# Causal-mask products by row groups, and block-scale steps moved from VectorE to ScalarE with new instruction orders, in a fused tokeniser, attention and feed-forward kernel

## The reference, cut to what matters

```
q, k = rotary(rmsnorm(x Wq)), rotary(rmsnorm(x Wk))      # 16 half heads of 16
scores = where(causal, q k / 4, -inf); attn = softmax(scores)
out = layernorm((attn[even] - lam * attn[odd]) v) * (1 - LAMBDA_INIT)
h2 = x + out Wproj
# feed-forward on layernorm(h2), every operand rounded in blocks of 16:
scale = max(max|block| / 6, 1e-12); q = grid(block / scale) * scale   # fp4 grid
y = h2 + (silu(q(x) q(Wg)) * (q(x) q(Wu)) -> q) q(Wd)     # 256 -> 704 -> 256
```

## Time and profile before

| | |
|---|---|
| median of 3 runs | 519.29 us (517.73 to 519.75) |
| profiled execution | 516.11 us, its span 514.4 us |
| granted TensorE clock, mean | 0.996 of full |
| busy PE / DVE / ACT / POOL | 483.8 / 465.5 / 327.7 / 263.7 us |

### The profile page before, as it was taken

One profiled execution on the slowest core, in us unless ns is written; L12 is line 12 of the kernel. 1 busy time (PEld: TensorE's weight loads), 2 busy tenths in 40 slices (PEclk: granted clock), 3 DMA queues, 4 the chain that ended last, 5 costly groups with the idle time before them and its releaser, 6 DMA issues.

```text
span 514.4 us, 13552 instructions
## 1 busy us (share of the span) xinstructions
PE 483.8 (94%) x3642; PEld 392.1 (76%) x3642; DVE 465.5 (91%) x1275; ACT 327.7 (64%) x752; POOL 263.7 (51%) x359
## 2 busy tenths in 40 slices
PE   4998998999999999999999979899999999999996
PEld 3776675677777777777776657798888888888895
DVE  4788989999999999999989799999999999999984
ACT  5787667687777877777776868554454454544531
POOL 4345545656454554454546245654565446556542
PEclk9999999999999999999999989999999999999999
DMA  8911101111111111111121111221212121121111
GB/s 283 351 50 44 34 2 38 58 46 50 55 54 48 48 47 49 54 52 48 48 61 43 48 39 30 60 63 51 61 42 60 52 61 52 50 61 53 51 45 56
DMA packets 31842, 32.12 MB, mean 62 GB/s; under 512 B 4160, under 2 KB 30016, under 8 KB 31808
## 3 DMA queue, kind: packets, MB, share of 16 engines
q1 hardware_dynamic: 31808, 31.72, 20.8%
HBM read 22.99 MB, written 8.71 MB: 62 GB/s over the span
## 4 chain that ended last, share of the span: by engine, by line
PE 47%; DVE 32%; issue 13%; DMA 2%; SPq 2%; ACT 1%; DVEq 1%; POOL 1%; POOLq 0%; ACTq 0%
PE bank L156 14%; PE bank_a L156 6%; PE bank L806 5%; PE bank L818 5%; DVE bank L1288 4%; PE bank L797 4%; DVE fh L1239 3%; DVE fh L1271 3%; PE bank L711 3%; DVE fh L1245 3%; PE bank L831 2%; PE bank_b L849 2%; DVE bank L1257 2%; DVE fx L1300 2%; DMA wproj_raw<-in_wproj_t 2%
## 5 line engine op out<-in xcount | busy, mean ns | idle before, releaser
L894 ACT ACTIVATE pt<-bank 113x452 f32<-113x452 f32 x128 | 61.0, 553 | 36.8 <-PE bank L806 36.8
L1361 POOL TENSOR_TENSOR h_deq<-fh,fhb 128x704 f32<-128x704 f32 (+1 forms) x29 | 39.6, 1366 | 62.2 <-DVE fhb L1213 61.0
L156 PE MATMUL bank<-wgu_hi,fx_hi 128*128 128x512 f32 x168 | 64.3, 383 | 1.8 <-DVE fx_lo L1280 1.8
L156 PE MATMUL bank<-wgu_hi,fx_lo 128*128 128x512 f32 x168 | 63.7, 379 | 0.0
L156 PE MATMUL bank<-wgu_lo,fx_hi 128*128 128x512 f32 x168 | 63.5, 378 | 0.0
L971 POOL TENSOR_TENSOR rope<-rope 113x512 f32<-113x512 f32 x32 | 41.0, 1283 | 30.3 <-DVE rope L1010 30.0
L964 POOL TENSOR_TENSOR rope<-rope,columns 113x256 f32<-113x256 f32 x64 | 48.2, 771 | 13.6 <-DVE rope L1002 13.1
L156 PE MATMUL bank_a<-wd_hi,fh_hi 128*128 128x256 f32 x168 | 49.8, 296 | 0.6 <-DVE fh_lo L1233 0.5
L156 PE MATMUL bank<-wqkv_hi,xo_hi 128*113 128x256 f32 (+1 forms) x128 | 46.6, 364 | 1.7 <-DVE rope L1002 1.5
L156 PE MATMUL bank_a<-wd_lo,fh_hi 128*128 128x256 f32 x168 | 46.9, 279 | 0.0
L156 PE MATMUL bank_a<-wd_hi,fh_lo 128*128 128x256 f32 x168 | 46.9, 279 | 0.0
(11 more groups left out here) (202 smaller groups left out, 1492.0 us busy)
## 6 DMA issues: line engine op xcount, KB each, us to landing
xb<-h_dram SPq DMA_DIRECT2D x29, 129.0 KB, 2.1
h_dram<-h SPq DMA_DIRECT2D x32, 112.9 KB
rb<-h_dram SPq DMA_DIRECT2D x28, 128.0 KB, 2.1
out<-res SPq DMA_DIRECT2D x28, 128.0 KB, 1.7
px<-in_patches SPq DMA_DIRECT2D x9, 384.0 KB, 9.2
hx<-in_txt SPq DMA_DIRECT2D x32, 77.0 KB
hr<-in_txt SPq DMA_DIRECT2D x32, 77.0 KB
h_dram<-y SPq DMA_DIRECT2D x9, 128.0 KB, 1.9
```

The costliest lines, as they stand in the source:

```text
L156: last = pe.matmul(dst, a(k), w(k), start=(start and n == 0), stop=(n == len(passes) - 1))
L894: act.activation(pt[0:T, r, :, :].rearrange("p s t -> p (s t)"), sc_ps[r][0:T, :], ACT.Exp, scale=1.0 / math.sqrt(HD)).then_inc(m["exp_mad ...
L1361: pool.tensor_tensor(blocks(of(h_deq, s), BLK), blocks(of(h_code, s), BLK), spread(of_blocks(h_scale, s), BLK), ALU.mult).then_inc(f["h_de ...
```

## The change

Masks: the mask tile becomes `late_16`, 32-row groups each holding the mask of four blocks of queries. The product is cut by query block g and row group r: 16 products with a contraction over 32 rows (17 in the last block).

```diff
-                for r in range(NG):
-                    pe.matmul(sc_ps[r][0:T, :], ident_16[0:T, 0:T], mask_16[0:T, :], start=True, stop=True)
+                if isinstance(s, int) and s == 0:
+                    pe.wait_ge(k["late_ready"], NG + 1)
+                for g in range(NG):
+                    queries = slice(g * ROW, min((g + 1) * ROW, T))
+                    wide = queries.stop - queries.start
+                    for r in range(NG):
+                        rows = slice(r * ROW, r * ROW + wide)
+                        pe.matmul(sc_ps[r][0:T, :].rearrange("p (s t) -> p s t", t=T)[:, :, queries], late_16[rows, g, :],
+                                  ident_16[rows, rows].unsqueeze(1).broadcast_to([wide, GS, wide]),
+                                  start=(g == 0), stop=True, skip_group_check=True)
```

Making the mask moves behind `b1_wide` on POOL, as one memset and four selections of 32 rows; PE's first wait no longer asks for it:

```diff
-            pool.memset(mask_16[:], 0.0).then_inc(k["ident_ready"], 1)
-            pool.wait_ge(k["ident_ready"], 9)
-            key_late = mask_16[0:T, :].rearrange("p (s t) -> p s t", t=T)
-            pool.affine_select(out=key_late, in_=key_late, compare_op=ALU.is_ge, fill=MASKED, base=0,
-                               pattern=[[0, GS], [1, T]], channel_multiplier=-1).then_inc(k["ident_ready"], 1)
             pool.wait_ge(k["columns_loaded"], 16)
             pool.tensor_copy(b1_wide[:], spread(columns[:, KP:2 * KP], P)).then_inc(k["b1_spread"], 1)
+            pool.memset(late_16[:], 0.0).then_inc(k["late_ready"], 1)
+            pool.wait_ge(k["late_ready"], 1)
+            for r in range(NG):
+                late = late_16[r * ROW:(r + 1) * ROW]
+                pool.affine_select(out=late, in_=late, compare_op=ALU.is_ge, fill=MASKED, base=0,
+                                   pattern=[[ROW, NG], [-1, T]], channel_multiplier=1).then_inc(k["late_ready"], 1)
+            pool.wait_ge(k["late_ready"], NG + 1)
```

```diff
+            def x_shorts(s):
+                ...
+                act.wait_ge(f["x_amax"], s + 1)
+                after(act, f["x_short"], s)
+                act.activation(x_over[:], x_amax[:], ACT.Relu, bias=below[:], scale=SHORT / 6.0).then_inc(f["x_over"], 1)
+                act.wait_ge(f["x_over"], s + 1)
+                after(act, f["x_inv"], s)
+                after(act, f["x_scaled"], s)
+                act.activation(x_short[:], x_over[:], ACT.Identity, bias=least[:]).then_inc(f["x_short"], 1)
+            def x_scales(s):
+                act.wait_ge(f["x_short"], s + 1)
+                after(act, f["x_deq"], s)
+                act.activation(x_scale[:], x_short[:], ACT.Copy, scale=-1.0 / SHORT).then_inc(f["x_scaled"], 1)
```

Orders: all lists from the transition on are new; the attention loop's are as before. The rounds of the feed-forward loop:

```diff
 SP
-                    (3, load), (-4, store), (-3, load_residual)))
+                    (4, load), (-4, store), (-3, load_residual)))
 DVE
-                    (-3, h_low), (2, x_maxima), (-4, rows_out), (2, x_inverse), (0, hidden), (-1, h_rounded),
-                    (1, x_low), (-1, h_codes), (2, x_rounded), (-1, h_scales), (2, x_codes), (0, h_maxima),
-                    (2, x_scales), (0, h_inverse)))
+                    (-1, hidden), (1, x_rounded), (-1, h_maxima), (1, x_codes), (-2, h_rounded),
+                    (-1, h_inverse), (-4, rows_out), (-3, h_low), (3, x_maxima), (-2, h_codes), (1, x_low),
+                    (3, x_inverse)))
 POOL
-                    (-2, h_dequantise), (1, x_dequantise), (-1, h_quotient), (2, x_quotient)))
+                    (2, x_quotient), (1, x_dequantise), (-1, h_quotient), (-2, h_dequantise)))
 ACT
-                    (-3, h_high), (2, x_norm), (0, silu), (-1, h_magnitude), (1, x_high), (2, x_magnitude)))
+                    (-1, h_shorts), (3, x_norm), (-3, h_high), (2, x_scales), (0, silu), (1, x_high),
+                    (3, x_shorts), (2, x_magnitude), (-1, h_magnitude), (-1, h_scales)))
 PE
-                    (0, first_columns), (0, middle_columns), (0, last_columns), (-2, h_transposes), (1, x_transposes), (-3, down)))
+                    (-4, down), (0, first_columns), (-3, h_transposes), (0, middle_columns), (1, x_transposes),
+                    (0, last_columns)))
```

More of the change, by code:

```diff
@@ L1318, in ffn_vector @@
-            return steps, namedtuple("FfnVector", "rows_out h_low h_rounded h_codes h_scales x_maxima x_inverse hidden x_low h_maxima h_inverse x_rounded x_codes x_scales")(rows_out, h_low, h_rounded, h_codes, h_scales, x_maxima, x_inverse, hidden, x_low, h_maxima, h_inverse, x_rounded, x_codes, x_scales)
+                    (-1, hidden), (1, x_rounded), (-1, h_maxima), (1, x_codes), (-2, h_rounded),
+                    (-1, h_inverse), (-4, rows_out), (-3, h_low), (3, x_maxima), (-2, h_codes), (1, x_low),
@@ L1339, in vector_transition @@
-            a.residual(30, 0); f.x_codes(3); f.x_scales(3); a.out_sums(30, 0); f.x_maxima(4); a.out_variance(30, 0)
-            f.x_inverse(4); f.h_rounded(1); f.hidden(2); f.x_low(3); f.h_codes(1); a.newton_step(35, 1)
-            f.h_scales(1); f.x_rounded(4); f.h_maxima(2); a.xo_low(36, 0); f.h_inverse(2); f.x_codes(4); f.h_low(0)
-            a.residual(31, 1); f.x_scales(4); a.out_sums(31, 1); f.x_maxima(5); a.out_variance(31, 1)
-            f.x_inverse(5); f.h_rounded(2); f.x_low(4); f.hidden(3); f.h_codes(2); a.newton_step(36, 0)
@@ L1344, in vector_transition @@
-            f.h_scales(2); f.h_maxima(3); f.h_inverse(3); f.x_rounded(5); f.h_low(1); f.x_codes(5); f.rows_out(0)
-            f.x_scales(5); f.hidden(4); f.h_rounded(3); f.h_codes(3); f.x_maxima(6); f.x_inverse(6); f.x_low(5)
-            f.h_scales(3); f.h_maxima(4); f.x_rounded(6); f.x_codes(6); f.x_scales(6); f.h_inverse(4)
+            a.out_variance(24, 0); a.ln_sums(31, 1); a.xo_low(30, 0); a.newton_step(29, 1); a.o_apply(26, 0)
+            a.scale_qk(29, 1); a.ln_variance(31, 1); a.ratios(27, 1); a.mix_product(27, 1); a.mix_sum(27, 1)
@@ new lines, in vector_transition @@
+            a.newton_step(35, 1); f.x_inverse(4); f.h_maxima(1); a.xo_low(36, 0); f.h_rounded(0); f.h_inverse(1)
+            f.x_maxima(5); f.x_low(3); a.residual(31, 1); a.out_sums(31, 1); a.out_variance(31, 1); f.h_codes(0)
+            f.hidden(2); f.x_rounded(4); f.x_codes(4); a.newton_step(36, 0); f.h_maxima(2); f.x_inverse(5)
+            f.h_rounded(1); f.h_inverse(2); f.h_low(0); f.x_low(4); f.h_codes(1); f.hidden(3); f.x_rounded(5)
+            f.x_codes(5); f.x_maxima(6); f.h_maxima(3); f.x_inverse(6); f.h_rounded(2); f.h_inverse(3)
@@ L1348, in ffn_gpsimd @@
+            f.rows_out(0); f.h_low(1); f.x_maxima(7); f.h_codes(2); f.x_low(5); f.x_inverse(7)
         def ffn_gpsimd(pool):
@@ L1809, in pipeline @@
             transition(engine, stages, tile_stages)
-            with engine.Fori(5, 24) as t:
+            with engine.Fori(5, 23) as t:
                 tiles(t)
```

252 lines of the change are left out of this document (130 added, 122 removed).

## The result

The changed kernel takes 512.38 us (median of 4 runs, 511.79 to 513.33), the kernel before 518.84 (4 runs, 517.73 to 519.75). The ratio is 0.9876 with a 95% interval of 0.9845 to 0.9908: faster by 1.2%. The forecast was 508.3, with a range of 503.0 to 517.5. The profiled execution took 512.66 us with a span of 510.9; that of before took 516.11 with 514.4.

What follows compares the result with a forecast made beforehand. PE was taken to bound the attention loop and DVE the feed-forward loop. Terms 2.7 + 1.4 + 5.9 + 1.8 - 0.5 - 0.3 = 11.0 us, off the 519.29 median, gave 508.3 us, range 503 to 517.5.

Steps and rivals of the forecast that it cites:

- its main term: Feed-forward loop: moved steps and new orders cut a tile from 7.24 to 6.92 us, gaining 5.9 us.
- the tightest ring: Feed-forward loop: waits from `h_maxima` through ACT and DVE back to it, 6.6 us, covered by PE's 6.92.
- The other terms: Gains of 2.7 and 1.4 from masks and 1.8 in the passage; losses of 0.5 at the start, 0.3 at the end.
- a kept pace: Rival, feed-forward loop: the tile stays at 7.24 us, 5.9 us is gone, total 514.2; 16 in 100.
- a ring slower than 7.24: Rival, feed-forward loop: the ring through `h_shorts` closes at 7.7 us, total 522.8; 9 in 100.
- the attention loop is PE's with DVE 0.19 behind: Attention loop: PE sets 7.02 us a sequence, and DVE lets only 0.19 us of any PE gain through.
- The terms 2.7 and 1.4: Mask gains: 2.7 us over the 18 looped sequences, 1.4 us over the other 14.
- The masks' price: Sixteen new mask products a sequence: 0.55 us taken, against 0.78 for the old four.
- The rival that they cost as much as the scores: Masks at the scores' 0.97 us add 0.19 a looped sequence on PE; total 517.2, no difference; 12 in 100.
- The passage: Between attention and feed-forward loops, 258 to 326 us: DVE spared small operations, 1.8 us gain counted.
- The end: Last stage: two ACT operations replace one on DVE for tiles 27 and 28, 0.3 us lost (0 to 1).
- The base: Whole kernel: 3.2 us added from the profiled 516.1 to the runs' median 519.29, moving 505.1 to 508.3.

Runs made afterwards that it cites:

- e1: The kernel before with only the new mask products and the mask made behind `b1_wide`; 518.26 us, ratio 0.9997 to the kernel before.
- e5: The changed kernel with its sixteen mask products issued three times over; 518.39 us in one run, the kernel before 517.19.
- e6: The changed kernel with `xo_high` copying only half its chunks in the attention loop, part of the computation left out; 511.3 us.
- e12: The changed kernel with the mask made ahead of `b1_wide`, `rope_sum(30)` ahead of `x_quotient(0)`, and filling transposes in passage and end; 509.17 us.
- e4: The changed kernel with the mask made ahead of `b1_wide`, as in the kernel before; 512.9 us.
- e10: The changed kernel with 11 filling transposes on TensorE ahead of `h_transposes(28)` at the end; 511.11 us.
- e9: The changed kernel with steps kept on ScalarE but the feed-forward orders of the kernel before on every engine; 569.69 us.
- e8: The changed kernel with its new orders, but the short and scale steps of the feed-forward part back on VectorE; 530.68 us.

## Why the prediction was right and where it failed

**The call, faster by over 0.5%, was right, and by its main term.** The feed-forward loop was DVE's, the moved steps and the new orders together hand it to PE, and the tile takes 6.89 us (forecast 6.92). 5.9 us were forecast and 6.3 came. The 5.9 was the old loop's 18.8 tiles times 0.32, which is 6.0. The price of ACT's six operations, the floor of PE, the tightest ring being covered, the later first `w_quotients` and that no table is loaded again in the loop were right. (That ring adds up to 6.7 with the 0.59 of `x_norm`, not to 6.6, and the prediction's 1.5 us from the Trainium skill's forms for the six operations is 1.64 by those forms; 1.71 came.) The other terms were to give 5.1 together; in the profiles they came to -2.8. That the measured median lies only 4.1 us above the forecast is owed in part to the base, as told below, and that part is luck. The rivals of a kept pace and of a ring slower than 7.24 fall with the 6.89.

**The failed step is "the attention loop is PE's with DVE 0.19 behind".** It rested on a chain of waits through PE alone. The loop is a ring through PE, ACT and DVE of 7.0 us, and PE's own work just filled it: the new masks take up to 0.26 us off PE and that changed nothing (e1), 0.45 more of them cost 0.22 (e5), and an ACT copy shorter by 0.19 gave 0.11 back until DVE's list held it (e6). The terms 2.7 and 1.4 hung on it; of 4.1 us some 0.4 at most came, start included. The profile of before had the row that would have told it: `xo_low` (L1025) ends at 207.92 and `project` starts at 207.98. I read only DVE's own idle time, and not who waits for DVE.

**The masks' price** was bounded from 0.40 to 0.97 and taken at 0.55. Their own row has 0.35; with the 0.09 by which they start later behind `qk_transposes` and the 0.08 or more by which `project` follows `pv_transposes` later, it is 0.52 or more, and PE's gain is 0.26 at most where 0.23 was forecast. So the term was sized well, and it was the path that gave nothing. By the Trainium skill's floor of about 25 ns between starts (TensorE: Matmul & The Clock Gate, Part 1) the sixteen alone would take 0.40 us; here they take 0.35, 22 ns each, and in e5 the 32 further ones take 0.45, 14 ns each; the chain has no 62 ns per product either. The prediction set its 0.2 us beside the drain at a change of tiling mode of which the Trainium skill, TensorEngine Tiling (Array Packing), Key Properties, speaks; that section gives no duration, so the two could not agree in size. The rival that they cost as much as the scores was wrong on that, and the outcome would have been the same had it been right within the shadow.

**The passage** was to gain 1.8 and lost 1.0, 1.7 for equal work. DVE had less to do there (61.13 us in place of 64.75 from 258 to 330 us), but the chain ran over ACT's table loads, POOL's quotient and a clock that was at its lower level twice and not once. e12's 70.8 us show that about 2 of these are to be had.

**The end** was to lose 0.3 and lost 2.2 in the profile, 1.4 of it in `down(27)` at the lower clock. Another 0.66 is `h_transposes(24)`, which the kernel before does ahead of the cut, so 0.1 is left. By the same cut e4 and e10 to e12 lose 0.2 to 0.5, less than those 0.66. So the two ACT operations cost nothing that shows here, and the low clock came in four of eight such profiles.

**The base.** The forecast went from one execution to the median of the runs by adding 3.2. It left open what made the difference, and the clock fits: over all chips the runs of the kernel before with a mean clock of 0.996 have spans of 514.5 to 515.5 us, those with 0.986 519.1 to 520.3. Its profiled execution was one of the first kind, the changed kernel's (0.99) wasn't. By the profiles 3.5 of the 11.0 us came, by the medians 6.5. The prediction had left the clock out, as "never under 0.97"; that was a mean over 68 us, and in the same profile it stands at 0.50 from 300 to 302 us.

## What to carry to other kernels

A chain of waits that names one engine isn't proof that it bounds a loop where the ends of its instructions are modelled: look, for each wait of that engine, when the other engine's last instruction ended, and whether the start always comes 0.05 us behind it. The gain of a stage isn't that of its own row either: here 0.17 of 0.43 us came back in the rows beside it. In a loop that is tuned close, several rings lie within 0.2 us of each other, and work taken off one engine or an order changed by hand runs into the next (7.00, 7.16 and 7.91 us here). A step moved to another engine needs an order that puts other work between its input and its use: without it the move lost some 51 us against the kernel before (e9). And an experiment that gives steps back must give them back as they were: e8's `scale` steps read another memory, stood behind POOL, and the experiment could not answer its question.

## What the runs showed of the hardware

- Sixteen products of 32 rows by 128 columns in four row groups take 0.35 us, less than half of the four whole ones that they replace (0.78), but the rows beside them become 0.17 us longer or more (e5). Thirty-two more of them take 0.45 us, 14 ns each (e5).
- A small operation on VectorE from an SBUF tile to another (128x44 or 128x16, fp32) that starts while a GpSimd multiplication runs ended 0.02 to 0.05 us after that multiplication, 29 of 29 times: 0.61 and 0.52 us (e8). Their like with an input in PSUM took 0.17 and 0.20 beside such a multiplication (kernel before).
- The granted clock fell to 0.50 for some 3 to 4 us after stretches in which TensorE stood still (2.0 of the 4 us before 280), but not each time: the same order at the end, with the same 1.7 to 1.8 us of standing, ran at the lower level in `down(27)` in four profiles (3.38 to 3.74 us) and at the upper in four (2.2 us). Where it falls differs between executions (280 to 286 and 314 to 320 us in the changed kernel, 304 to 310 in e10, whose order up to there is the same). What decides it isn't shown.
- A difference of 0.01 in the mean clock of a run goes with 4 to 6 us of span in the kernel before (514.5 to 515.5 us at 0.996, 519.1 to 520.3 at 0.986), most of its spread from run to run; not all, as its runs at 0.99 have 518.0 to 520.7.
